# Decay attention of a two-layer language-model tower: steps of two heads and four sequences in 64-query blocks

## The reference, cut to what matters

```python
def _forward(x, ...):                 # x = _layernorm(h), 8 heads of 8
    low = causal_conv(x, conv_w, taps=5) + conv_b
    hid = _layernorm(low + sqrt_beta**2 * (x - low) + x, ln_w, ln_b)      # eps 1e-12
    q, k, v = proj(q_w, q_b), proj(k_w, k_b), proj(v_w, v_b)
    scores = q @ k.T / sqrt(8)
    p_ = softmax(where(mask, scores, -1e32)) * mask
    dist = sqrt(clip((p_.sum(-1) - cumsum(p_)) * abs(i - j), 0))
    effect = clip(exp(dist * -softplus(gammas)), 1e-5, 1e5)
    p = softmax(where(mask, scores * effect, -1e32)); p[query 0] = 0
    return (p @ v) @ out_w.T + out_b
```

## Time and profile before

| | |
|---|---|
| median of 3 runs | 3456.83 us (3451.32 to 3473.36) |
| the profiled execution | 3448.74 us, of which the span of its instructions 3446.8 us |
| mean granted TensorE clock in it | 0.945 of 2.4 GHz |
| decay attention, first load to last addition | 1760 to 3252 us of the span |
| busy over the span | PE 92%, DVE 66%, ACT 52%, POOL 40% |

### The profile page before, as it was taken

One profiled execution on the slowest core, in us unless ns is written; L12 is line 12 of the kernel. 1 busy time (PEld: TensorE's weight loads), 2 busy tenths in 40 slices (PEclk: granted clock), 3 DMA queues, 4 the chain that ended last, 5 costly groups with the idle time before them and its releaser, 6 DMA issues. The chain is left out here.

```text
span 3446.8 us, 63508 instructions
## 1 busy us (share of the span) xinstructions
PE 3178.7 (92%) x21487; PEld 2207.0 (64%) x21598; DVE 2279.0 (66%) x4822; ACT 1790.9 (52%) x3588; POOL 1376.8 (40%) x1488
## 2 busy tenths in 40 slices
PE   7995899965999999999979999999999999999676
PEld 6885677743555555555546777777777777777455
DVE  4994677756444444444436888888888888888633
ACT  1441566642333322333315777777777777777542
POOL 5650344431000000000004666666666666666461
PEclk9996899977999999999977999999999999999887
DMA  1110000000000000000000000000000000000002
GB/s 44 39 37 6 2 2 2 2 24 1 1 0 0 0 0 0 0 0 0 0 11 1 1 0 0 0 0 0 0 0 0 0 0 0 0 0 0 3 1 49
DMA packets 30290, 19.39 MB, mean 6 GB/s; under 512 B 24011, under 2 KB 27532, under 8 KB 30181
## 3 DMA queue, kind: packets, MB, share of 16 engines
q0 software_dynamic: 6144, 9.84, 1.2%
q1 hardware_dynamic: 24036, 8.12, 1.0%
HBM read 13.75 MB, written 4.19 MB: 5 GB/s over the span
## 5 line engine op out<-in xcount | busy, mean ns | idle before, releaser
L1245 DVE TENSOR_TENSOR prod<-c_h,act 128x512 f32<-128x512 f32 x352 | 243.3, 691 | 480.9 <-PE c_h L1097 396.8
L1177 ACT ACTIVATE act<-c_h 128x512 f32<-128x512 f32 x352 | 210.1, 597 | 655.8 <-PE c_h L1097 655.8
L1430 POOL TENSOR_TENSOR d_decay<-d_later,d_pos 128x512 f32<-128x512 f32 x256 | 326.0, 1273 | 474.5 <-DVE d_later L1847 474.5
L1124 PEld LDWEIGHTS c_out<-e_w,hid 128*128 128x128 f32 x2816 | 340.6, 191 | 79.5 <-issue 79.3
L1124 PE MATMUL c_out<-e_w,hid 128*128 128x64 f32 x2816 | 388.8, 281 | 0.1
L1847 DVE TENSOR_TENSOR_SCAN d_later<-d_cont,d_ex 128x512 f32<-128x512 f32 x256 | 315.8, 1234 | 49.6 <-ACT d_ex L1712 46.2
L1071 POOL TENSOR_TENSOR x_rest<-flatT,x_hm 64x512 f32<-64x512 bf16 (+1 forms) x33 | 38.1, 1154 | 748.5 <-ACT x_hm L1157 724.6
L1548 PEld LDWEIGHTS d_S<-d_kT,d_qT 8*128 8x128 f32 x2048 | 249.4, 188 | 110.6 <-issue 110.6
L1548 PE MATMUL d_S<-d_kT,d_qT 8*128 8x128 f32 x2048 | 298.4, 285 | 0.0
L1439 POOL TENSOR_TENSOR d_p<-d_p,d_mx 128x512 f32<-128x512 f32 x256 | 266.0, 1039 | 60.0 <-DVE d_mx L1866 58.7
L1542 PE MATMUL d_S<-d_hide,d_ident_b 128*128 128x512 bf16 x1088 | 281.7, 384 | 0.0
(11 more groups left out here) (323 smaller groups left out, 6556.7 us busy)
## 6 DMA issues: line engine op xcount, KB each, us to landing
out_h<-g_Y SPq DMA_DIRECT2D x8, 512.0 KB, 4.0
rows<-in_table,idx POOLq DMA_INDIRECT x128
e_w<-in_e_w SPq DMA_DIRECT2D x2, 704.0 KB
e_w<-in_e_w SPq DMA_DIRECT2D x1, 352.0 KB
d_pos<-in_d_pos SPq DMA_DIRECT2D x1, 256.0 KB
d_cont<-in_d_cont SPq DMA_DIRECT2D x1, 256.0 KB
g_w<-in_g_w SPq DMA_DIRECT2D x3, 64.0 KB, 2.0
d_win<-in_d_win SPq DMA_DIRECT2D x1, 146.2 KB
```

Of the source, the lines that this page charges most:

```text
L1124: last = nc.tensor.matmul(bo[:, b * D:(b + 1) * D], hid[u][:, b * P:(b + 1) * P], w2[:, c, :], start=(c == 0 and b == 0), stop=(c == NCH - ...
L1245: nc.vector.tensor_tensor(prod[u][:], b3[u][:], act1[u][:], ALU.mult).then_inc(S["multiplied"], 1)
L1430: pool.tensor_tensor(decay[u][:], later[u][:, 0:W], pos[:], ALU.mult).then_inc(S["placed"], 1)
```

## The change

The phase is written anew. One step is now two heads (e) of one group: 128 steps. The 128 partitions hold 64 queries of two sequences. A step's tile has per head 384 elements: two "long" pieces of 128 keys (the second 64 queries of the two pairs of sequences, S=1) and two "short" pieces of 64 keys (the first 64 queries, S=0, which see only 64 keys). Every elementwise operation runs over both heads at once where it can, and as a long and a short instruction where a value per piece enters. There are 2 slots (2 PSUM banks each), the masking matmul is issued once per head, and nothing overwrites it. `-softplus(gamma)` is squared and folded into the distances once (posg), so the third exp has the constant scale -1. Weights are block-diagonal (`twice`), so two sequences go through one matmul of 128 rows: convolution 10 matmuls 128x128 a group, projections 256 columns. The mean subtraction after the convolution is folded into its weights; LayerNorms run as whole-group instructions over [128, 4, 64] on VectorE, ScalarE and GpSimd. The loop is gone: each engine's queue is written out for K = -16 to 136.

The order of the queues in step K, cut to its core (j = K % 4; n is a group):

```diff
+ # POOL, step K
+ scaled(K-1): long(decay) *= rtot ; short(decay) *= rtot        # after inv_total, placed
+ shifted2(K-2): long(p2) -= mx2 ; short(p2) -= mx2
+ j==0: hTr (two reversed copies), mean*1/D, hc = H - mean ; j==1: H += cb
+ j==2: hn = zb * rstd2, xn = hc * rstd
+ placed(K): decay = later * posg                                # after scanned(K), weighed(K-2)
+ # PE, step K
+ if K >= 2: pe.wait_ge(U["weighed"], K - 1)
+ for e in range(2):
+     nc.tensor.matmul(bS[u][:, e, 0:SEG], ident_b[:], hide[:], start=True, stop=False)
+ for g, S in ((0, 1), (1, 1), (0, 0), (1, 0)):
+     for e in range(2):
+         r = slice(STRIP * (j % 2 * 2 + e), STRIP * (j % 2 * 2 + e) + 2 * HD)
+         last = nc.tensor.matmul(bS[u][:, e, cols], qT[s][r, c, ...], kT[s][r, c, keys], ...)
+ turn(K-3, 0)                                                   # 3 transposes
+ j==0: q projection, convolution ; j==2: v projection
+ odd K: values((K-5)//2)         # 32 matmuls of 64 columns, 4 column strips, 4 heads
+ turn(K-3, 1)                                                   # after pT_kept of turn(K-3, 0)
+ j==1: k projection ; j==2: turn y ; j==3: turn x, turn h, output projection
+ odd K: turn back (4 transposes)          # after attT_kept and both pT_kept
+ # ACT, step K
+ Ln(K-1), Exp(K-1, 0.5), Exp of ex (K), Exp(K-1, -1.0)
+ keep_turned(K-3, 0), Exp of p2 (K-2)
+ j==0: two q copies, square ; odd K: attT ; keep_turned(K-3, 1)
+ j==0: square ; j==1: k copy, 4 small ; j==2: v copy, yT ; j==3: xT, hT
+ # DVE, step K
+ max long, max short, subtract long, subtract short (K)         # after scored(K)
+ even K: reciprocal and product of y ; j==1: two reduces
+ scan(K)                                                        # after exped(K), 768 elements
+ two reciprocals (K), weigh (K-1), max2 long, max2 short (K-1)
+ j==0: zb ; j==3: H += out, reduce for the mean
- for _ in range(AGAIN[k % GQ]):
-     nc.tensor.matmul(bS[u][:], ident_b[:], hide[:, None, :].to_broadcast([P, GB, P]), start=True, stop=True)
- with eng.Fori(1, TURNS) as i:
-     for k in range(TURN):
-         body(i, k, -TURN, TURN)
```

The value matmuls and one of the split elementwise operations, word for word:

```diff
+ def weigh_values(g, S):
+     rows = slice(0, P) if S else slice(g * HALF, (g + 1) * HALF)
+     for side in range(2):
+         b = 2 * g + side
+         at = (g * P if S else 2 * P) + side * HALF
+         for e in range(QUAD):
+             last = nc.tensor.matmul(bO[e * STRIP:(e + 1) * STRIP, b * P + S * HALF:b * P + (S + 1) * HALF],
+                                     vs[rows, b if S else GB + side, QUAD * c + e, :],
+                                     pT[(QUAD * i + e) % KEEP_T][rows, at:at + HALF], start=True, stop=True)
+ def long(tile):
+     return tile[:, :, 0:2 * P].rearrange("p e (g t) -> p e g t", t=P)
+ def wide(small, which, width):
+     return small[:, which][:, :, :, None].to_broadcast([P, 2, 2, width])
+ pool.tensor_tensor(long(decay[u]), long(decay[u]), wide(rtot[u], 1, P), ALU.mult)
```

More of the change, by code:

```diff
@@ new lines, in turn_pairs, with project @@
+                def turn_pairs(bank, at, tile, made):
+                    for g in range(2):
+                        last = nc.tensor.transpose(bank[:, at + g * P:at + (g + 1) * P],
+                                                   tile[:, 2 * g:2 * g + 2, :].rearrange("p b d -> p (b d)"), ident[:])
+                    last.then_inc(G[made], 1)
+                def project(bank, which, rows):
+                    for c in range(2):
+                        cols = slice((2 * which + c) * P, (2 * which + c + 1) * P)
+                        out = bank[:, c * 2 * P:(c + 1) * 2 * P]
+                        nc.tensor.matmul(out, bias[:, cols], ones[:], start=(c == 0), stop=False)
+                        last = nc.tensor.matmul(out, wqk[:, cols], rows, start=False, stop=(c == 1))
+                    return last
@@ L1586, in body @@
+                    if K % 2 and quad_there(i):
+                        pe.wait_ge(Q["attT_kept"], i + 1)
+                        if step_there(K - 3):
+                            pe.wait_ge(U["pT_kept"], 2 * (K - 2))
+                        if i >= 1:
+                            pe.wait_ge(Q["y_made"], i)
                         for b in range(GB):
@@ L1873, in body @@
-                    beside(i, k, work)
-                work = Work()
-                pipeline(body, dve, work)
-        m.clear_semaphores()
+                    if j == 1:
+                        n = m + 3
+                        if there(n):
+                            dve.wait_ge(G["squared"], n + 1)
+                            after(dve, "log_var", n - 1)
+                            nc.vector.tensor_reduce(ss[:], sq[:], AX, ALU.add).then_inc(G["spread"], 1)
+                        n = m + 2
+                        if there(n):
+                            dve.wait_ge(G["squared2"], n + 1)
+                            after(dve, "log_var2", n - 1)
+                            nc.vector.tensor_reduce(ss2[:], sq2[:], AX, ALU.add).then_inc(G["spread2"], 1)
@@ L2260, in lay_out, with twice, strips @@
-    a["d_cont"] = np.tile((np.arange(W) % P != 0), (P, 1)).astype(np.float32)
-    a["d_hide"] = np.where(j > i, -1e32, 0.0).astype(np.float32)
-    a["d_notfirst"] = (i > 0).astype(np.float32)
-    a["ident64"] = np.eye(D, dtype=np.float32)
+    def twice(w):
+        both = np.zeros((P, P), np.float32)
+        both[:D, :D] = both[D:, D:] = w
+        return both
+    def strips(w):
+        w = w.reshape(D, 2, 4, 8)
+        both = np.zeros((2, D, 2, 4, 4, 8), np.float32)
+        for c in range(2):
+            both[c, :, :, :, c] = w
+        return both.reshape(P, 2 * P)
@@ new lines, in strip_rows @@
+    def strip_rows(v):
+        v = v.reshape(2, 4, 1, 8)
+        return np.concatenate([np.repeat(v, 2, 2), np.zeros((2, 4, 2, 8), np.float32)], 2).reshape(1, 2 * P)
+    taps = g["L1_attn_conv_w"].transpose(1, 2, 0)
+    a["d_conv"] = np.stack([twice(taps[:, t]) for t in range(taps.shape[1])], 1)
+    a["d_convb"] = np.tile(g["L1_attn_conv_b"][None], (P, 1))
+    a["d_beta"] = np.tile(g["L1_attn_sqrt_beta"].reshape(1, D), (P, 2))
+    a["d_wqk"] = np.concatenate([strips(g[f"L1_attn_{c}_w"].T) for c in "qk"], 1)
@@ new lines, in lay_out @@
+    ahead = np.concatenate([np.tile(D + q - far, (1, 2)), np.tile(q - near, (1, 2))], 1)
+    a["d_pos"] = np.maximum(ahead, 0).astype(np.float32)
+    a["d_hide"] = np.where(ahead < 0, -1e32, 0.0).astype(np.float32)
+    first = np.zeros(3 * P, np.float32)
+    first[[0, P, 2 * P, 2 * P + D]] = 1
+    a["d_cont"] = np.tile(1 - first, (P, 2))
+    a["d_notfirst"] = (np.arange(P)[:, None] > 0).astype(np.float32)
+    row = np.arange(P)[:, None] % 32 // 8
+    a["d_half"] = (row == np.arange(2)[None]).astype(np.float32)
```

950 lines of the change are left out of this document (465 added, 485 removed).

## The result

| | before | after |
|---|---|---|
| median of 4 runs each, same chip | 3463.64 us | 3349.23 us (3325.11 to 3391.95) |
| ratio to before, 95% interval | | 0.965 (0.958 to 0.972) |
| profiled execution, span | 3448.74, 3446.8 us | 3346.25, 3344.5 us |
| granted TensorE clock, whole span | 0.945 | 0.806 |
| decay attention, first load to last addition | 1491.5 us | 1368.8 us |

What follows compares the result with a forecast made beforehand. TensorE was taken to bound the old kernel, at 10.97 us for two heads; loops between engines would set the new step. 60 + 128 x 8.7 + 27 = 1200.6 us instead of 1491.5, -291, gave 3160 us, range 3070 to 3350.

Steps and rivals of the forecast that it cites:

- The step at full clock: One new step, two heads of a group, scan to scan: 8.4 us with TensorE at full clock.
- 60 + 128 x 8.4 + 27: Decay attention phase: 60 us ahead of the first scores, 128 steps of 8.4 us, 27 us behind them.
- Loop A: Scan to next scan through placed, scaled, Ln and root, and the next exp: 7.77 us, 8.0 with hand-overs.
- GpSimd's standstill beside the scan: GpSimd's group work stands still while VectorE's scan reads two SBUF tiles: mean +0.3 us a step.
- one step in four to three at the half clock, +0.3: TensorE's granted clock in the steps: this share at half clock raises the step from 8.4 to 8.7 us.
- the 1.2 us taken: Masking and scores on TensorE at half clock: 1.2 us longer a step.
- some 0.5 us late: Odd steps at full clock: transposes back, ahead of the next scores, wait for ScalarE's second copy and end this late.
- rival 1: TensorE's clock stays at half throughout the phase: 10.4 us a step, 3375 us; chance 0.13.
- rival 2: GpSimd's four-dimensional operands cost double in scaled and shifted2: 10.0 us a step, 3324 us; chance 0.12.
- Rival 4: TensorE's strips don't run side by side for scores and values: 13.1 us a step, 3721 us; chance 0.07.
- Rival 3: Nothing stands in the way, full clock, no sharing, values at 1.0 us: 8.0 a step, 3068 us; chance 0.15.
- the 0.15 that the forecast tried: Draining TensorE at each tiling change, 0.15 us: 1.5 us of TensorE work, 9.0 us a step; nothing added.

Runs made afterwards that it cites:

- e4_before_unfilled: The kernel before without its 1088 overwritten masking matmuls; 3590.86 us against 3493.34 on that chip, ratio 1.031.
- e3_filled: The changed kernel plus overwritten masking matmuls in TensorE's two gaps, 10 on even steps and 8 on odd; 3122.37 us, ratio to before 0.898.
- e1_y_first: The changed kernel with only the reciprocal and product of y moved ahead of the maxima on VectorE; 3238.57 us, ratio to before 0.934.
- e5_order: The changed kernel with y ahead of the maxima on VectorE and ScalarE's copies moved earlier, nothing filled; 3310.60 us, ratio to before 0.954.
- e8_y_first_filled: e3_filled with y moved ahead of the maxima, ScalarE's copies left in place; 3155.85 us, ratio to before 0.912.
- e9_exp_first_filled: e3_filled with the exp of the current step moved ahead of the previous step's Ln and root on ScalarE; 3313.75 us, ratio to before 0.962.

## Why the prediction was wrong, point by point

- **The bound of before: right in its effect, half right in its cause.** TensorE was full, and 281.7 us of it was overwritten masking. The forecast counted these as ballast of which the change rids itself. e4_before_unfilled shows that without them the old kernel is slower.
- **Prices: right.** Scan 1.759 us (forecast 1.77), product with distances 1.815 (1.82), scaling 1.039 and 0.612, weighing 0.925, exp 0.84. At full clock masking holds TensorE 0.43 us and the scores 1.03 (2411.25, 2411.68, 2412.71 in e3_filled; forecast 0.40 and 1.05). 32 value matmuls take 1.37 us at full clock; the forecast put 2.0 into its sum, which cost it nothing, since TensorE's total does not set the step there.
- **The step at full clock: right.** Forecast 8.4, measured 8.23 to 8.26 at 0.96; the phase of e3_filled takes 1137.2 us (1766.75 to 2903.94), where 60 + 128 x 8.4 + 27 gives 1162. Loop A is 7.92 us (8.0), and GpSimd's standstill beside the scan is there, at j=0 as forecast.
- **The clock: this is the step that failed.** "I take one step in four to three at the half clock, +0.3" is wrong in both factors: the share of time at half clock and the price of a step at it. The share at half is about three quarters, not one quarter. And a step at half costs more than the 1.2 us taken, which were masking and scores alone. By the three points above, 0.55 us per tenth, a step wholly at half clock costs by estimate some 2.8 us more than one at full. With the order of the queues left alone, the clock took 10.09 - 8.25 = 1.84 us a step instead of 0.3, which is 1.54 too much, and the whole miss is 10.09 - 8.7 = 1.39, since the step at full clock came out 0.15 shorter than forecast.
- **Why the price was too low.** The forecast gave odd steps "some 0.5 us late" by the order of times at full clock. Masking and scores did lengthen by the 1.2 us taken (0.49 to 0.85 and 1.11 to 1.97), but at half clock the rest of TensorE's step stands in the loop too: the masking started 2.46 us after its slot was free (2505.50 - 2503.04). VectorE's wait for scores (277.9 us over 120 steps, 2.3 each) goes with that. The loop was not worked out at half clock.
- **Feedback.** The forecast argued against rival 1 that longer steps fill TensorE again, so the clock should rise. They did not: TensorE is 75% busy and stays at 0.63. In the changed kernel a slow clock lengthens the step and the other engines' waits with it, and TensorE's gaps stay.
- **Rival 1 comes nearest to what happened,** with 10.4 us and 3375 us forecast, 10.09 and 3349 measured, though the clock is at half for three quarters of the time and not always. It had a chance of 0.13. The earlier trace rows held the warning, 10 of 10 us busy at clock 0.50. That the time still lies inside the range, 1 us under its end, is luck: the range reached up to 3350 on account of rival 2, which did not occur. Its chances do not add up either: rivals 1 and 4, both above 3350, have 0.22 together where the range leaves 0.13.
- **Rival 2 is out:** GpSimd's four-dimensional operands cost 1.039 us for 512 elements, as before. **Rival 4 is out:** scores on two row strips take half of eight times 0.27, values pack on four column strips, as forecast. **Rival 3,** 8.0 a step, needs the fill, and even then is missed by 0.2.
- **Changing between tilings does cost, and the forecast read the earlier trace rows wrongly when it found nothing beyond the work.** In the kernel before, overwritten masking matmuls of 512 columns start 0.216 us apart, but the last of them and the first score matmul, on a row strip, 0.309; in e3_filled the same two distances are 0.163 and 0.256 for 384 columns. From the last transpose to the next matmul of full rows are 0.109 us, to the first value matmul on a column strip 0.202. Each change seen costs about 0.09 us at full clock, less than the 0.15 that the forecast tried. The Trainium skill (TensorEngine Tiling (Array Packing), Key Properties) says that changing the tiling mode drains TensorE; these distances agree with it in that every change seen costs time. The step at full clock still came out right because the prices from the earlier trace rows were taken start to start and so contain such changes.
- **Order:** real, but smaller than the clock. Without fill moving y alone gives 0.83 us a step; with fill it gives nothing at best (8.22 at 0.92 against 8.23 at 0.96), and costs 0.3 with the fill of e3_filled.

What stays open: how much of the 0.83 us of e1_y_first comes from the wait itself and how much from the convolution's falling into the full-clock stretch. e5_order points to the clock: there too y is first and its wait nearly gone, but the convolution is still mostly at half clock,

```profile
L1531 PE MATMUL d_X<-d_conv,d_xT 128*128 128x128 f32 x420 | 76.4, 363 | 0.0
```

and the interval from the scan of j=0 to that of j=1 stays at 11.59 us (11.50 in the changed kernel, 8.08 in e1_y_first). In e3_filled, with the convolution at full clock and a wait for y of 1.0 us, it is 8.59. Since e5_order also moved ScalarE's copies, and the fill shortens the wait, this is a sign and not a proof. Why the granted clock falls where it does is not worked out here either.

## What to carry to other kernels

Before you book the removal of overwritten or otherwise idle TensorE work as a gain, ask what the clock does without it, and work out every loop at both clock levels; the loop that is longest at half clock may be one that is harmless at full. A mean clock is not enough for this: see which matmuls get the full clock. Where a kernel goes from a full TensorE to a chain of hand-overs, put cheap overwritten matmuls into the gaps ahead of waits (here 9 a step took 7% off the kernel), and try several amounts and places. Moving an operation forward in a queue helps only if its input is there: both rearrangements of ScalarE's queue tried here merely took a wait to the head of a queue that others stand behind.

## What the runs showed of the hardware that was not expected

- In e8_y_first_filled and e9_exp_first_filled the granted clock is the same (0.85) and the steps are 8.54 and 9.67 us: a mean clock is no measure of a schedule. In e1_y_first against after it is nearly the same (0.66, 0.63) with 0.83 us between the steps.
- Averaged over 800 us, the granted clock follows the fill in degrees (0.63, 0.77, 0.96 for no, half and full fill), while the clock record holds only the two levels, 1.2 and 2.4 GHz: eight score matmuls take 1.97 us (2506.27) or 1.11 (1840.09).
- A GpSimd subtraction that takes 0.61 us alone takes 2.15 beside a scan, longer than the scan itself (1.76). The forecast expected it to stand still meanwhile; it loses 1.54 us, 88% of the scan.
- A change between tilings of TensorE costs about 0.09 us from one start to the next at full clock (0.309 against 0.216, 0.202 against 0.109).
- A quarter of the time idle on TensorE (914.39 of 1220 us busy) went with 0.63, and 15% idle (682.15 of 800) with 0.96; but 3% idle in e4_before_unfilled (774.35 of 800) went with only 0.81. The longest gap does not tell it either: in these windows 0.88 us in e4_before_unfilled and 1.50 in e3_filled. Neither the busy share of the records nor the gaps alone tell the clock from one kernel to another.
